# Abs, Sign and the weight-quantizer's front ahead of the attention tile, and the FFN quantizer's front ahead of the MLP tile, in an eight-core layer kernel

## What is computed

```python
x = L0_attn_x                                   # (2, 8192, 1024) f32
xn = _layernorm(x)
# attention branch
qkv = rmsnorm(xn) @ qkv_w.T; q, k = exp(-0.5*q*q), exp(-0.5*k*k)     # 16 heads of 64
kv = sum over rows of k (x) v;  out = q @ kv / (q . sum k)
x1 = xn + gamma * (out @ proj_w.T + proj_b)
attn = x1 + gamma * (gelu(rmsnorm(x1) @ conv1_w.T + b1) @ conv2_w.T + b2)   # hidden 2048
# FFN branch; fq() is the FP4 quantize-dequantize, scale = max(|block of 16|)/6
h = silu(fq(xn) @ fq(w_gate).T) * (fq(xn) @ fq(w_up).T)              # width 2816
y = x + attn + fq(h) @ fq(w_down).T
```

## Time and profile before

| what | value |
|---|---|
| timed runs (2) | 4016.97 and 4054.72 us, median 4035.84 |
| profiled execution | 4013.58 us, span of its slowest core 4012.0 us |
| spans of the cores | 3984.7 to 4012.0 us |
| mean granted TensorE clock | 0.705 to 0.707 of full speed |
| busy: PE, DVE, ACT, POOL | 41%, 55%, 20%, 16% of the span |
| stage A / stage B2 | about 95 to 1250 us / 1892 to 2705 us |

### The profile page before, as it was taken

How to read it: one execution, slowest core, us unless ns; L and a number is a source line. 1 busy time by engine, 2 the same in 40 slices (tenths; PEclk the granted TensorE clock), 3 DMA queues, 4 the chain that set the end, 5 groups by cost and what they waited for, 6 DMA issues and landing times.

```text
span 4012.0 us, 28638 instructions; the slowest of 8 cores (3984.7 to 4012.0 us)
## 1 busy us (share of the span) xinstructions
PE 1635.1 (41%) x7488; PEld 716.1 (18%) x7488; DVE 2197.6 (55%) x3809; ACT 784.8 (20%) x1179; POOL 648.4 (16%) x381
## 2 busy tenths in 40 slices
PE   0545444447783233301334443441533432432069
PEld 0222222223331111100111111110211111110024
DVE  2667676766632455512766666540576677667401
ACT  0333333334442000000111111110211211211000
POOL 0122112111100000000211111100323323323100
PEclk9777777778897666655666666665766766766579
DMA  4121211112212312135011111108000000000563
GB/s 157 48 71 55 69 56 68 56 61 79 79 56 63 82 68 71 51 103 142 33 58 59 56 59 47 52 34 157 8 15 7 15 15 8 15 15 8 95 155 105
DMA packets 225800, 245.71 MB, mean 61 GB/s; under 512 B 173284, under 2 KB 173284, under 8 KB 224614
## 3 DMA queue, kind: packets, MB, share of 16 engines
q1 hardware_dynamic: 214086, 211.37, 18.3%
q10 hardware_dynamic: 11520, 32.51, 2.0%
q0 software_dynamic: 32, 0.00, 0.0%
HBM read 135.85 MB, written 66.58 MB: 50 GB/s over the span
## 4 chain that ended last, share of the span: by engine, by line
DVE 41%; PE 22%; DMA 13%; issue 10%; ACT 5%; SPq 4%; POOL 3%; DVEq 1%; ACTq 0%; POOLq 0%
PE KV L920 4%; DVE q_m L376 4%; DMA xb<-x_all 4%; DVE q_lt L373 3%; DMA wldB<-conv_wT 3%; DVE q_amax L330 3%; PE PA L994 2%; DVE q_m L400 2%; DVE q_m L388 2%; DVE q_m L394 2%; DVE q_g L409 2%; DVE q_m L382 2%; DVE q_m L406 2%; DVE q_lt L385 2%; DVE q_lt L397 2%
## 5 line engine op out<-in xcount | busy, mean ns | idle before, releaser
L355 POOL TENSOR_TENSOR q_ss<-q_sgn,q_hs 128x1024 f32<-128x1024 f32 (+1 forms) x140 | 262.3, 1874 | 2542.2 <-DVE q_hs L346 1381.4
L994 PE MATMUL PA<-wgT,xqTall 128*128 128x512 bf16 x384 | 115.7, 451 | 626.0 <-ACT hsila L1008 540.2
L373 DVE TENSOR_SCALAR q_lt<-q_a 128x1024 bf16<-128x1024 f32 (+1 forms) x140 | 135.5, 968 | 316.8 <-POOL q_a L360 316.8
L360 POOL TENSOR_TENSOR q_a<-q_a,q_inv 128x1024 f32<-128x1024 f32 (+1 forms) x140 | 278.4, 1989 | 0.0
L565 PE MATMUL PA<-wTs,xTb 128*128 128x512 bf16 x256 | 133.9, 523 | 230.4 <-ACT xTb L561 230.4
L565 PE MATMUL PA<-wTs,xTa 128*128 128x512 bf16 x256 | 121.4, 474 | 259.4 <-ACT xTa L561 259.4
L994 PEld LDWEIGHTS PA<-wgT,xqTall 128*128 128x128 bf16 x384 | 41.1, 110 | 687.4 <-issue 659.5
L376 DVE TENSOR_SCALAR q_m<-q_a 128x1024 bf16<-128x1024 f32 (+1 forms) x140 | 162.6, 1161 | 0.0
L326 ACT ACTIVATE q_a<-wqld 128x1024 f32<-128x1024 f32 x76 | 71.9, 946 | 375.0 <-DVE xqB L412 183.8
L1072 PE MATMUL PA<-wdT,hqTall 128*128 128x512 bf16 x176 | 71.2, 405 | 171.0 <-DMA hqTall<-hqspill 171.0
L565 PE MATMUL PB<-wTs,xTb 128*128 128x512 bf16 x256 | 131.6, 514 | 0.0
(11 more groups left out here) (234 smaller groups left out, 4447.2 us busy)
## 6 DMA issues: line engine op xcount, KB each, us to landing
xb<-x_all SPq DMA_DIRECT2D x64, 512.0 KB, 3.9
wldB<-conv_wT SPq DMA_DIRECT2D x32, 512.0 KB, 3.6
wld<-qkv_wT SPq DMA_DIRECT2D x8, 1536.0 KB, 6.5
wqld<-w_gate SPq DMA_DIRECT2D x22, 512.0 KB, 4.4
wqld<-w_up SPq DMA_DIRECT2D x22, 512.0 KB, 4.3
wqld<-w_down SPq DMA_DIRECT2D x16, 704.0 KB, 5.4
hqspill<-hq ACTq DMA_DIRECT2D x16, 704.0 KB, 3.1
wgq<-wqout SPq DMA_DIRECT2D x22, 256.0 KB, 2.2
```

Source lines behind the costliest of these rows:

```text
L355: oprw(p, 'gpsimd', lambda g, NB=NB, W=W, sgn=sgn, hs=hs, ssb=ssb: g.tensor_tensor(ssb.ap[:, 0:W].rearrange("p (a b) -> p a b", b=QB), sgn ...
L360: oprw(p, 'gpsimd', lambda g, NB=NB, W=W, inv=inv, qa=qa: g.tensor_tensor(qa.ap[:, 0:W].rearrange("p (a b) -> p a b", b=QB), qa.ap[:, 0:W] ...
L373: oprw(p, 'vector', lambda g, W=W, q_a=q_a: g.tensor_scalar(q_lt.ap[:, 0:W], q_a.ap[:, 0:W], 0.25, None, ALU.is_gt), reads=[q_a], writes=[ ...
L994: oprw(p, 'tensor', lambda T, kc=kc, occ=occ, w=w, pg=pg, t=t: T.matmul(pg.ap[:, 0:w], xqTallC[kc].ap[:, kc * S_core + t * 128:kc * S_core ...
```

## The change

Two moves of calls in the emission order; no instruction is added, removed or resized.

In stage A the front of the weight job is emitted ahead of `stageA2(t)` instead of after `stageA2kv(t-1)`. In stage B2 `stageB2a(t+1)` is emitted first in the iteration, ahead of `stageB2m(t)` and `stageB2c(t-1)`, instead of behind them.

```diff
@@ -635,12 +635,12 @@
             stageA1a(t + 2)
         if t + 1 < T_batch:
             stageA1b(t + 1)
+        if (t < 34 or t % 2 == 0) and w_pre < min(len(wjobs), 44):
+            emit_wjob_pre(w_pre)
+            w_pre += 1
         stageA2(t)
         if t > 0:
             stageA2kv(t - 1)
-        if (t < 34 or t % 2 == 0) and w_pre < min(len(wjobs), 44):
-            emit_wjob_pre(w_pre)
-            w_pre += 1
         if wj_i < w_pre - 1:
             emit_wjob_main(wj_i)
             wj_i += 1
@@ -937,11 +937,12 @@
     stageB2a(0)
     stageB2oai(0)
     for t in range(T_own):
+        if t + 1 < T_own:
+            stageB2a(t + 1)
         stageB2m(t)
         if t > 0:
             stageB2c(t - 1)
         if t + 1 < T_own:
-            stageB2a(t + 1)
             stageB2oai(t + 1)
         stageB2q(t)
         if wj_i < len(wjobs):
```

## The result

The changed kernel takes 4171.4 us, median of 11 runs (4157.5 to 4192.1), against 4018.1 us for the kernel before in the same series: ratio 1.0366, 95% interval 1.0331 to 1.0400. The forecast was 4170 and slower. Executions in which one die (cores 0 to 3 or 4 to 7) took over 1% longer than the other at a lower granted clock are left out of the medians and ratios. The profiled execution has a span of 4162.8 us (core 0 is the slowest of 8; core 2 was in the profile before), 150.8 us more than before. Both edits cost time, each for itself.

The account below looks back on a forecast made before the run. No engine is full, so each stage is a loop of waits (stage A: DVE work plus one load). 89 + 20 - 14 + 62 = +157 on the profiled 4013.6 us gave 4170 us, range 4100 to 4220.

Parts of the forecast that it names:

- Stage A, price: Stage A: GpSimd's two passes under the first comparisons of each main cost DVE 3.43 us a job.
- (d): Rival, 4217 us: 4.1 us a job in stage A and a late load in B2; chance 0.08.
- (c): Rival, 4026 us: stage A mains run unslowed once L373 starts ahead of q_ss; chance 0.07.
- (e): Rival, 3914 us: stage A mains without slowdown, B2's x_own load landed ahead of W; chance 0.03.
- Stage A, sum: Stage A's 33 tiles: 113 us of new overlap less 24 of old overlaps gone, +89 (bounds +31, +118).
- Pairs: Stage A from tile 34, nine pairs with a job in every second tile: +20 us (0 to +30).
- Start: Start of stage A: job 1's weights load earlier, its reduce near 103 us instead of 118.7; -14 us (0 to -16).
- Stage B2: B2: Gelus, PE and L930 queue behind Abs, waiting for L868; 12 x 19.1 + 2 x 2.2 - 14 x 12.2 = +62 us.
- W: B2: end of the job's last L412, before which the x_own load can't start; second L930 forecast 24.3 us later.
- upper bound of +95: B2: the sum if each job's load is late by the rest of its margin.
- Rival (b): B2 breaks even, 4109 us: chain from L868 to second L930 5.2 us shorter, by higher clock or early Gelus; chance 0.14.
- some 11 us: B2, a sign of the forecast: L930 waits some 11 us for PE.

Follow-up runs that it names:

- e3b_qa_held: e3_pool_held with only GpSimd's second pass (q_a) held until DVE's main is over, q_ss beside L373 as in the changed kernel; 4108.2 us.
- e7_after_first: e3_pool_held with GpSimd's two passes held only until L373, the first comparison of the main, is over; 4167.9 us.
- e3_pool_held: Changed kernel with GpSimd's two passes of a stage A job held until DVE's last instruction of the main; 4032.1 us.
- e4_act_behind: Changed kernel with Abs, Sign and GpSimd's passes in B2 behind the hdT copies, x_own load and DVE's part staying ahead; 3999.2 us.
- e5_xown_early: Changed kernel with B2's x_own load issued a whole tile earlier, ACT's order unchanged; 4130.0 us.
- e6_all: Changed kernel with the edits of e3_pool_held, e4_act_behind and e5_xown_early together; 3846.4 us, ratio 0.954.

## Why the prediction was right

**Stage A, price.** 3.43 us a job from the earlier trace rows held to the hundredth (434.26 to 438.83), because the rows had the same engines, tiles and order. e3b_qa_held shows what it is made of, and e7_after_first that its place in the row doesn't matter. It is 1.7 for each GpSimd instruction, which takes 1.93 us with no DVE instruction beside it (616.20 and 618.09 in e3_pool_held). In the changed kernel's tile L373 ends at 436.57 and L376 at 438.91, each 0.55 us after the GpSimd pass beside it (436.02, 438.36); q_a takes 2.38, 0.45 more than alone, and its first 0.59 us lie beside L373. What in the chip makes them hold each other up was not shown. For (d), 4217, and so for the top of the range, the author counted 4.1 us a job, both GpSimd lengths of the earlier trace rows less the lead of 0.17; no run shows that term, the traces have 3.43. Nor does a run show the mains without slowdown on which the 50 us rest that (c), 4026, and (e), 3914, take off in stage A: with L373 first, e7_after_first has q_ss at 2.12 us instead of 1.93 and L379 at 2.42 instead of 0.68.

**Stage A, sum.** 113 - 24 = 89, measured 89.1. The 24 were 13.8, 5.0 and 5.3. The price came in 32 of the 33 tiles on L373 and L376; in the first of them Sign ended later, and q_ss and q_a stretched L394 and L397 instead. The copy of xT 2 us later was costed at nothing with ACT's and PE's slack as cover; e3_pool_held shows it is nothing. Pairs: +20, measured +22.0.

**Start.** -14, measured -17.8 over the first four tiles. The mechanism was right: Sign of job 0 now ends at 103.3 and the load of job 1 is issued at once. The reduce of job 1 came at 108.7, not near 103: on this core the stage itself began 4.5 us later, and the L543 ahead of it took 1.93 us beside GpSimd instead of 0.81, the 1 us of new overlap. The other 3.3 us are the main of job 0: GpSimd's passes of job 1 fell into it before (L379 to L409 took 10.8 us in all) and don't after (7.5). They fall into the next main now, the first of the 33, so this part was moved, not saved. The same place shows a DVE instruction that GpSimd left alone:

```profile
104.43 1.92 POOL L355 TENSOR_TENSOR q_ss<-q_sgn,q_hs 128x1024 f32<-128x1024 f32 x1 [102.22 <-DVE q_hs L346]
...
105.39 0.69 DVE L517 BATCH_NORM_STATS2 mva<-xb 128x6 f32<-128x512 f32 x1
...
106.87 1.93 DVE L543 TENSOR_SCALAR xn1c<-xb,mvc 128x1024 bf16<-128x1024 f32 x1
```
The bn_stats L517 beside q_ss takes 0.69 us, as it does at 428.21 with no GpSimd pass beside it.

**Stage B2.** The mechanism was right in each step, and its sum 10 us too large (62 against 52.3). W to the second L930: 24.3 forecast, 24.2 here, mean a little less. L868 stands 4.40 behind W in the mean, where 4.74 was taken from a load issued behind another store: 12 x 0.34 = 4. From the L930 to the job's reduce 10.81 against 11.13, as xqB's L412 no longer has the 0.35 of idle time it had in the old period: 14 x 0.3 = 4. L868 to the second L930 took 18.2 to 19.9 us (19.57 forecast), mean 19.4: 12 x 0.16 = 2. Together that is the 10. The three periods without a job and the end behind them came to -34.0 against -32.2. The upper bound of +95 needed a late load of the job's weights; the reduce never waits for it in B2. In e4_act_behind the same working gave 22.6 and the trace 22.2.

**The total.** 4170 against 4171.4 is closer than the parts are, and that is luck. From profile to profile the change cost 150.8 us where 157 were forecast. B2 came out 10 us lower, the start 4 lower, the pairs 2 higher, the untouched stretches and the start of the program 5 higher together, and the median of the changed kernel lies 9 above its own profiled span. Rival (b) asked for L930 without its wait, (d) for a late load in B2 and (e) for an x_own load landed ahead of W; none is in the trace. Matmuls at a higher clock, which could have shortened (b)'s chain, are not there either: between hdT and the second L930 the granted clock was 0.50 for most of the first 16 and 1.00 behind them before (2216 to 2224, 2224 to 2230 us), 0.50 and 0.96 after (2486 to 2491, 2491 to 2496). DVE's wait for PE at the first L930, forecast as "some 11 us", was 11.9.

## What to carry to other kernels

A call moved ahead in the emission order moves ahead on every engine at once. Work out for each in-order queue what it now stands in front of: DVE's front could go first at a gain, while ACT's two short instructions behind it kept four Gelus, and PE's 32 matmuls behind those, waiting for a load.

Put GpSimd's elementwise passes into DVE's waits, not beside its comparisons. One wait on DVE's last instruction was worth 139 us here.

## What the runs showed that was not expected

A GpSimd pass of 1.93 us lengthened one comparison on DVE by 1.7, at the head of DVE's row (L373 2.31 instead of 0.63, L376 2.42 instead of 0.68, changed kernel) and inside it (L379 and L382 2.42, e7_after_first); there it was not kept out for the length of the row. GpSimd's own passes took up to 2.39 us in the changed kernel and 2.48 in e7_after_first. Stretched elsewhere: L412 2.90 instead of 1.23, L543 1.93 instead of 0.81. The bn_stats L517 kept its 0.69 us beside GpSimd. At L412, the last of the row, the kernel before shows both cases. With q_ss 0.11 us ahead of it, L412 took 2.90 us and q_ss 1.93; with q_ss 0.04 us behind it (508.80 against 508.76), L412 kept 1.23 and q_ss took 2.98.

With less time in stages A and B2, F1 and F2 took 24 (e5_xown_early) and 35 us (e6_all) longer on the slowest core, at a granted clock of 0.80 (3910 to 4124 us, core 1) and 0.73 (3612 to 3845 us, core 5) in F2, against 0.92 on core 4 and 0.89 on core 0 of the same runs. It isn't the work of all cores that grew. In all four executions of e6_all one die has a mean granted clock of 0.70 to 0.71 and holds the slowest core; the other has 0.72, and its slowest core ends at 3804 to 3812 us, where 3818 was forecast. In e5_xown_early the dies differ in three of four executions, and the better one ends at 4096 to 4102, where 4116 was forecast. So what is missing at the end goes with the lower clock of one die and not with the edits' sums. In e4_act_behind, with B2 shortened by 153 us, F1 and F2 took 11 us less, so a shorter B2 alone doesn't bring it about. What lowers the clock is open.
